# Attention and routed experts on one core: unscaled probabilities, the inverse sums spread by TensorE and applied to the output

## What is computed

```python
qkv = jnp.einsum('bsm,qhdm->bqhsd', x, W_qkv)
qk_rot = qk * cos + _rotate_half(qk) * sin
scores = jnp.einsum('bhqd,bhkd->bhqk', Q, K)
scores = jnp.where(causal, -jnp.inf, scores) / sqrt(DK)
attn = jax.nn.softmax(scores, axis=-1)
out = jnp.einsum('bhqk,bhkd->bhqd', attn, V)
out = out.transpose(0, 2, 1, 3).reshape(B, S, H * DK)
return jnp.einsum('bsh,dh->bsd', out, W_o)
...
x = x + _L0_attn_ref(xn, L0_attn_W_qkv, L0_attn_W_o) + _L0_ffn_ref(xn, ...)
```

## Time and profile before

| | |
|---|---|
| median of 3 runs | 1601.31 us (1599.42 to 1608.61) |
| profiled execution | 1614.56 us, span 1612.7 us |
| TensorE busy | 1267.3 us (79%) |
| VectorE busy | 1155.0 us (72%) |
| ScalarE busy | 1123.7 us (70%) |
| GpSimd busy | 971.7 us (60%) |
| granted TensorE clock, mean | 0.942 of full speed |

### The profile page before, as it was taken

How to read it: one execution, slowest core, us unless ns; L and a number is a source line. 1 busy time by engine, 2 the same in 40 slices (tenths; PEclk the granted TensorE clock), 3 DMA queues, 4 the chain that set the end, 5 groups by cost and what they waited for, 6 DMA issues and landing times.

```text
span 1612.7 us, 46469 instructions
## 1 busy us (share of the span) xinstructions
PE 1267.3 (79%) x13108; PEld 874.4 (54%) x13109; DVE 1155.0 (72%) x4320; ACT 1123.7 (70%) x3606; POOL 971.7 (60%) x1579
## 2 busy tenths in 40 slices
PE   2415877788778878878699999888888888888888
PEld 1303544455444545555498899655555555555555
DVE  6787766666666666667377777777778787877776
ACT  6415666666666767667588888777778777767777
POOL 3245676767677767677200000488778787878776
PEclk9657999999998999999799999999999999999999
DMA  9612222222231322222333323234333333433341
GB/s 288 182 42 63 66 67 65 66 59 72 61 69 44 67 64 65 66 65 67 102 84 85 88 85 85 65 85 96 72 72 74 72 74 74 95 76 75 78 95 33
DMA packets 115784, 129.10 MB, mean 80 GB/s; under 512 B 11568, under 2 KB 75312, under 8 KB 115376
## 3 DMA queue, kind: packets, MB, share of 16 engines
q1 hardware_dynamic: 107056, 110.26, 28.5%
q0 software_dynamic: 8576, 17.33, 3.7%
HBM read 28.85 MB, written 31.59 MB: 37 GB/s over the span
## 4 chain that ended last, share of the span: by engine, by line
POOL 30%; PE 20%; issue 18%; DMA 17%; DVE 11%; ACT 2%; DVEq 1%; POOLq 1%; ACTq 0%; SPq 0%
DMA sorted_x_dram<-stage,rows_at 11%; POOL probs L478 7%; POOL probs L479 7%; PE bank L1081 5%; PE bank L1082 5%; DMA stage<-sorted_y_dram,rows_at 5%; PE bank L1083 4%; POOL arena L462 4%; POOL stage L489 4%; POOL sorted_x_dram L483 3%; POOL arena L461 3%; PE bank L1162 1%; PE bank L1152 1%; PE bank L1216 1%; DVE arena L951 1%
## 5 line engine op out<-in xcount | busy, mean ns | idle before, releaser
L624 ACT ACTIVATE probs<-arena,neg_max 128x128 f32<-128x128 f32 (+1 forms) x1024 | 453.6, 446 | 186.9 <-DVE neg_max L951 178.5
L1162 PE MATMUL bank<-ident,probs 128*128 128x128 f32 x1536 | 276.1, 290 | 165.5 <-POOL probs L479 140.2
L478 POOL TENSOR_TENSOR probs<-probs,inv_total 128x128 f32<-128x128 f32 x512 | 217.1, 424 | 229.6 <-DVE inv_total L958 127.2
L1162 PEld LDWEIGHTS bank<-ident,probs 128*128 128x128 f32 x1536 | 174.9, 145 | 272.6 <-issue 136.1
L951 DVE CUSTOM_DVE_ANT_0 arena<-bank,causal 128x128 f32<-128x128 f32 (+1 forms) x1024 | 315.8, 345 | 2.7 <-PE bank L1152 2.7
L489 POOL DMA_INDIRECT stage<-sorted_y_dram,rows_at x128 | 134.5, 1050 | 263.1 <-DMA sorted_y_dram<-stage 241.4
L479 POOL TENSOR_SCALAR probs<-probs,inv_total 128x256 f32<-128x256 f32 x512 | 274.6, 536 | 0.0
L1152 PE MATMUL bank<-arena 64*128 64x128 f16 (+1 forms) x3072 | 177.1, 250 | 50.6 <-DVE neg_max L951 47.2
L969 DVE TENSOR_TENSOR arena<-bank,arena 128x256 f16<-128x256 f32 x256 | 106.5, 416 | 133.2 <-ACT arena L616 122.3
L624 ACT ACTIVATION_READ_ACCUMULATOR probs<-arena,neg_max 128x1 f32 x1024 | 194.5, 190 | 0.0
L611 ACT ACTIVATE probsT<-bank 128x384 f32<-128x384 f32 x384 | 184.3, 480 | 10.4 <-PE bank L1162 10.2
(11 more groups left out here) (149 smaller groups left out, 2971.4 us busy)
## 6 DMA issues: line engine op xcount, KB each, us to landing
arena<-arena SPq DMA_DIRECT2D x256, 256.0 KB, 5.1
arena<-sorted_x_dram SPq DMA_DIRECT2D x72, 128.0 KB, 2.2
sorted_y_dram<-stage SPq DMA_DIRECT2D x72, 128.0 KB, 1.8
sorted_x_dram<-arena SPq DMA_DIRECT2D x3, 2304.0 KB, 17.9
arena<-experts_dram SPq DMA_DIRECT2D x8, 512.0 KB, 5.1
out_dram<-acc SPq DMA_DIRECT2D x32, 128.0 KB
sorted_x_dram<-arena SPq DMA_DIRECT2D x1, 2368.0 KB, 19.1
sorted_x_dram<-stage,rows_at POOLq DMA_INDIRECT x128, 2.4
```

The costliest lines, as they stand in the source:

```text
L478: nc.gpsimd.tensor_tensor(p0, p0, inv_total[:, s % 4, 0:1].broadcast_to([P, P]), ALU.mult)
L624: last = nc.scalar.activation(probs[:, s % 4, at:at + w], masked[:, s % 2, at:at + w], ACT.Exp, bias=neg_max[:, s % 2, t:t + 1], scale=-1. ...
L1162: last = nc.tensor.transpose(TP[s % 2][:, k * P:(k + 1) * P], probs[:, s % 4, k * P:(k + 1) * P], ident[:])
```

## The change

Probabilities are no longer scaled. A transpose waits for the exponential alone. VectorE takes the reciprocal of the sums for a pair at once, four steps after its scores, and makes two f16 parts of it (high and low, times 64). TensorE multiplies each part, spread over 64 columns, by an f16 unit matrix, so that the inverse of a token's sum stands in PSUM in each of its head's 64 rows (`turn_sums`, eight products a pair). ScalarE copies the output to SBUF whole (`o_copy`), VectorE multiplies it by the inverse one step later (`o_scale`), and GpSimd splits it in two f16 parts after another step (`o_split`). The product with V moves from the end of the even step to directly behind the scores, with the spreading products behind it. The sends move to odd steps only, one gather moves from step 10 to 9, and the dispatch of rows is done in two halves, at steps 0 and 8. There are four buffers for masked scores instead of two.

```diff
-SEND_AT = [1, 3, 5, 7, 9, 11, 12, 14]
-GATHER_AT = [1, 3, 5, 7, 9, 10, 11, 13]
+SEND_AT = [1, 3, 5, 7, 9, 11, 13, 15]
+DISPATCH_AT = [0, 8]
+GATHER_AT = [1, 3, 5, 7, 9, 9, 11, 13]
-INV_LAG, T_LAG, OUT_LAG, PV_LAG, O_LAG = 2, 3, 4, 5, 6
+T_LAG, OUT_LAG, INV_LAG, PV_LAG, O_LAG, SCALE_LAG, SPLIT_LAG = 3, 4, 4, 5, 6, 7, 8
...
+        INV = [b[:, SEQ:2 * SEQ] for b in bank[6:8]]
...
-            def scale(G, s):
-                pool.wait_ge(inv_done, G + 1)
-                p0, p1 = probs[:, s % 4, 0:P], probs[:, s % 4, P:PW]
-                nc.gpsimd.tensor_tensor(p0, p0, inv_total[:, s % 4, 0:1].broadcast_to([P, P]), ALU.mult)
-                nc.gpsimd.tensor_scalar(p1, p1, inv_total[:, s % 4, 1:2], 1.0, ALU.mult, ALU.mult).then_inc(p_ready, 1)
+            def o_split(J, j, parity):
+
+                pool.wait_ge(o_scaled, J + 1)
+                nc.gpsimd.tensor_tensor(pause[:], half[:, 0:1], half[:, 0:1], ALU.add)
+                hi, lo = ot_hi[parity][:, j, :], ot_lo[parity][:, j, :]
+                nc.gpsimd.tensor_copy(hi, o_whole[:, j % 2, :]).then_inc(o_hi, 1)
+                pool.wait_ge(o_hi, J + 1)
+                nc.gpsimd.tensor_tensor(lo, o_whole[:, j % 2, :], hi, ALU.subtract).then_inc(o_done, 1)
...
+                    if sends:
+                        i = SEND_AT.index(s)
+                        if i % PER == 0:
+                            pool.wait_ge(send_ready, 2 * b + i // PER + 1)
+                        if not (at == OPENING and i == 0):
+                            pool.wait_ge(sent, 16 * (PER * TOP * b + i))
...
-            def o_high(G, s, parity):
-
-                act.wait_ge(pv_done, G + 1)
-                nc.scalar.activation(ot_hi[parity][:, s // 2, :], PV[s // 2 % 2], ACT.Copy).then_inc(o_hi, 1)
+            def o_copy(J, j):
+
+                act.wait_ge(inv_turned, J + 1)
+                if not (isinstance(J, int) and J < 2):
+                    act.wait_ge(o_done, J - 1)
+                nc.scalar.activation(o_whole[:, j % 2, :], PV[j % 2], ACT.Copy).then_inc(o_out, 1)
...
-                G = 16 * b + s
-                dve.wait_ge(s_ready, 8 * b + s // 2 + 1)
-                if not (at_fill and s < INV_LAG):
-
-                    invert(G - INV_LAG, s - INV_LAG)
+                if s % 2 == 0:
+                    dve.wait_ge(s_ready, 8 * b + s // 2 + 1)
+                    if not (at_fill and s < INV_LAG):
+
+                        invert(8 * b + (s - INV_LAG) // 2, (s - INV_LAG) % H // 2)
...
+                if s % 2 == 0 and not (at_fill and s < INV_LAG):
+                    split_inverse(8 * b + (s - INV_LAG) // 2, (s - INV_LAG) % H // 2)
...
+            def split_inverse(J, j):
...
+                nc.vector.tensor_scalar(hi, inv, W_SCALE, None, ALU.mult).then_inc(inv_hi, 1)
+                dve.wait_ge(inv_hi, J + 1)
+                nc.vector.scalar_tensor_tensor(lo, inv, W_SCALE, hi, ALU.mult, ALU.subtract).then_inc(inv_ready, 1)
...
-            def o_low(J, s, parity):
-                dve.wait_ge(o_hi, J + 1)
-                j = s // 2
-                nc.vector.tensor_tensor(ot_lo[parity][:, j, :], PV[j % 2], ot_hi[parity][:, j, :], ALU.subtract).then_inc(o_done, 1)
+            def o_scale(J, j):
+                dve.wait_ge(o_out, J + 1)
+                dve.wait_ge(inv_turned, J + 1)
+                nc.vector.scalar_tensor_tensor(o_whole[:, j % 2, :], INV[j % 2], UNSCALE, o_whole[:, j % 2, :],
+                                               ALU.mult, ALU.mult).then_inc(o_scaled, 1)
...
             def transposes(G, s, free):
-                pe.wait_ge(p_ready, G + 1)
+                pe.wait_ge(exp_done, G + 1)
...
+            def turn_sums(b, j):
+
+                pe.wait_ge(inv_ready, 8 * b + j + 1)
+                for t in range(TPS):
+                    for l in range(2):
+                        for i in range(2):
+                            of = inv_parts[:, l, 2 * j % SUMS + i, t:t + 1].broadcast_to([P, DK])
+                            last = mm(INV[j % 2][64 * i:64 * i + 64, t * P:(t + 1) * P], of, ident_h[:], start=(l == 0), stop=(l == 1))
+                last.then_inc(inv_turned, 1)
...
-                    pe.wait_ge(o_done, 8 * b + j - 1)
+                    pe.wait_ge(o_scaled, 8 * b + j - 1)
...
+                    if ends:
+                        attend(ended[0], ended[1] // 2, at)
+                        turn_sums(ended[0], ended[1] // 2)
```

More of the change, by code:

```diff
@@ L513, in sample @@
                         send(SEND_AT.index(s))
-                    if gathers:
-                        gather(GATHER_AT.index(s))
+                    for k in gathers:
+                        gather(k)
             def rest_of(b):
-                for lag in range(INV_LAG, 0, -1):
-                    scale(16 * b + 16 - lag, H - lag)
+                for s in range(H, H + SPLIT_LAG):
+                    if (s - SPLIT_LAG) % 2 == 1:
+                        o_split(8 * b + (s - SPLIT_LAG - 1) // 2, (s - SPLIT_LAG) // 2, b % 2)
             former_samples(pool, sample)
@@ L863, in tile_slots, with dispatch @@
                 return slots[:, first:first + n, :] if isinstance(first, int) else slots[:, bass.ds(first, n), :]
-            def dispatch(b):
+            def dispatch(b, part):
                 if not (isinstance(b, int) and b == 0):
-                    dve.wait_ge(sent, 16 * PER * TOP * b)
-                for t in range(PER):
+                    dve.wait_ge(sent, 16 * PER * (TOP * b + part - 1))
+                n = PER // 2
+                for t in range(n * part, n * part + n):
                     tile = b * PER + t
@@ L1185, in sample @@
                         scores(b, s, parity, at == OPENING)
+                    ended = (b, s - PV_LAG) if s > PV_LAG else (b - 1, s - PV_LAG + H)
+                    ends = ended[1] % 2 == 1 and not (at in FILLS and s <= PV_LAG)
+                    if ends:
+                        attend(ended[0], ended[1] // 2, at)
+                        turn_sums(ended[0], ended[1] // 2)
                     for kind, j, u, psum, n in beside(b, at, s):
```

110 lines of the change are left out of this document (60 added, 50 removed).

## The result

The changed kernel takes 1659.12 us (median of 4 runs, 1659.0 to 1665.9) against 1604.74 us for the kernel before in the same session: 1.035 times as long (95% interval 1.031 to 1.040). I had said 1584 us, within 1546 to 1626. The change made the kernel 3.5% slower and fell outside the range.

The account below looks back on a forecast made before the run. No engine was full; waits bound it: GpSimd's send-scaling-transpose chain in former samples, VectorE in the rope half. Latter +8, former -29, ends +4 gave -17 us, about 1584 us; overall range 1546 to 1626, forecast's own 1568 to 1598.

Parts of the forecast that it names:

- products that spread the inverse: TensorE, eight products per pair, 256 pairs: 0.31 us a group, 2.5 us a sample, on the path only where TensorE limits.
- every rival: Four other outcomes: waits go everywhere 0.16, sends bind 0.17, VectorE's even step decides 0.14, spreading products dear 0.11.
- Sum: Whole kernel: latter samples +8, former samples -29, ends +4, together -17 us on 1614.56 us, or -1.05%.
- Former sample: Each sample of the sending half: -1.8 us, from 41.0 to near 39.2 us.
- Latter sample: Each sample of the half without sends: +0.5 us, from 36.9 to near 37.4 us.
- Dear: Rival on TensorE's spreading products: 0.75 us a group instead of 0.31, kernel at 1612 us; chance 0.11.
- VectorE's even step: Rope half: forecast +0.2 us a pair, 5.0 us; as rival, up to 0.65 us a pair, 1640 us, chance 0.14.
- the gathers: One gather moves from step 10 to 9, odd-step gathers start later: set against each other at -0.3 us a sample.
- The part for the scale: VectorE's output multiplication, moved from an odd step into the even step inside the loop: some 0.35 us a pair.
- Ends: End of either half, where nothing hides the longer tail of copy, scale, split and output product: +2 us twice.
- the pairs at 10 and 12 of a former sample: Sign of a right forecast: these pairs take near 5 us, though send landings still last up to 6 us.
- two halves: Dispatch of rows in a former sample stays: four operations of 0.34 us, some 1.1 us in two halves.

Follow-up runs that it names:

- e9: Changed kernel with 24 tiny products put in once in the first sample, ahead of the former loop, loop bodies untouched: 0.992, 1597.7 us.
- e2: Changed kernel without the low part of the inverse in the spread, four spreading products a pair instead of eight: 0.992, 1595.5 us.
- e5: Kernel before with four unread products of nine columns by one ahead of each product with V: 1.004.
- e6: Kernel before with nine unread products of nine columns by one ahead of each product with V: 1.006, 1617.4 us.
- e11: Kernel e3 with VectorE's output scale moved to the next odd step and GpSimd's split one step later: 0.949, 1526.4 us.
- e3: Changed kernel with both loops over samples written out, with no jumps: 0.966, 1557.4 us.
- e13: Kernel e6 with 18 of its tiny products taken out of the first sample, ahead of the former loop: 1.046, 1678.5 us.
- e10: Kernel e2 with 19 tiny products put in once in the first sample, ahead of the former loop: 1.000.
- e4: Kernel before with both loops over samples written out, with no jumps: 0.971, 1566.1 us.

## Why the prediction was wrong

**The step that failed** is the bullet on the products that spread the inverse. It priced eight products a pair, 256 pairs, by their time on TensorE alone (0.31 us a group, and that part was right: 0.33 us), and so did every rival. The sum had no term for their number: 16 instructions a pair, with the waits 278 more in a body of two samples, in a program of which that body is run seven times in each half. Both bodies then touched 8 blocks of 256 instructions instead of 7 and were fetched anew at every jump: 61 us that the sum had at nothing.

What it costs, from the changed kernel against e9: a former sample 40.97 us against 38.84, a latter one 39.30 against 37.39, over 15 samples each 32 + 29 = 61 us, or 5.1 us at each of the twelve jumps. 4.9 us of that is seen directly as the two stands of TensorE; the clock at 0.50 behind them adds to it, and waits that the jump had anyway (VectorE's "issue" of 2.3 to 3.1 us at e9's latter jumps is gone in the changed kernel, where VectorE waits for the scores) take from it. What share each has wasn't taken apart.

The Trainium skill ("Runtime: NRT & Kernel Launch", section "Instruction fetch mechanics") could have warned me that a loop's size can cost. It says that instructions come in blocks of 16 KiB, 256 instructions, that TensorE's memory for them is 128 KiB (eight such blocks), and that a jump whose target isn't in the current window of two pages must wait for a DMA of it. The packets here are 2.38 MB / 145 = 16.4 KB, and the limit lies where eight blocks would put it, if one of the eight is taken by the block fetched ahead: seven stay, eight don't, and nine packets come per iteration. That last picture is my reading of the counts; no run tests it. As to the window of two, here bodies of seven blocks jumped back without a single packet (e2, e5, e6, e9), so for TensorE the measurement decides against it.

**What held.** e9 is the changed kernel without the penalty, and can be set against each term:

- *Sum.* -17 us forecast on the profiled execution's time; e9's is 1597.8 against 1614.56, -16.8 us. That they agree so closely is luck: these are single executions of two sessions. The medians of e9's session are 1597.72 and 1608.38, -10.7 us, and its ratio says -0.8%, forecast -1.05%.
- *Former sample* forecast 39.2 us, e9 38.8. *Latter sample* forecast 37.4, e9 37.4.
- *Spreading products* forecast 0.31 us a group; measured 1132.52 to 1132.85 and, in e9, 1251.91 to 1252.25: 0.33 and 0.34 us. Leaving half of them out, with both bodies loaded, changes nothing (e2 0.992, e9 0.992). "Dear" was wrong, and the spacing of 81 ns of the Trainium skill ("TensorE: Matmul & The Clock Gate", section "Back-to-back issue gap") isn't met here either (0.33 us for eight is 41 ns each).
- *VectorE's even step*, 5.0 us forecast for the pair at 4, +0.2 us for each of the pairs at 2 to 8. In e9 the scores of one latter sample, the pairs at 4, 6 and 8 and the start of 10:

```profile
1339.49 0.67 PE L1192 MATMUL bank<-arena 64*128 64x128 f16 x12
1344.75 0.67 PE L1192 MATMUL bank<-arena 64*128 64x128 f16 x12 [0.33 <-DVE neg_max L975]
1349.44 0.67 PE L1192 MATMUL bank<-arena 64*128 64x128 f16 x12 [0.33 <-DVE neg_max L975]
1354.59 0.67 PE L1192 MATMUL bank<-arena 64*128 64x128 f16 x12 [2.05 <-DVE neg_max L975]
```

  5.26, 4.69 and 5.15 us. Taken as means over the fourteen samples of the latter loop (distances between the starts of the scores), the pairs at 2 to 8 make 19.4 us against 18.1 before: +1.3 where I said +0.9. The pairs at 10 to 14 make 13.2 against 13.9, -0.7, which is what the sum had for them with the gathers (+0.9 - 1.3 - 0.3). The part for the scale, 0.35 x 4 = 1.4 us a sample, equals what e11 gives back in a latter sample (36.0 - 34.6), but not in the place where I put it: from e3 to e11 the pairs at 2 to 8 lose only 0.5 us, and those at 10 to 14 lose 0.8, beside the shorter waits for gathered rows. In a former sample 0.5 comes back, and nothing of it in the pairs at 2 to 8. So 0.35 us a pair for the scale is not confirmed.
- *Ends* were under-priced: +4 us forecast. From the last former to the first latter sample 284.3 us against 280.6, and from the last sample's mark to the end 39.6 against 35.1: +8 us, paid for by the former samples.

**What was right in sum and wrong in place.** I expected the pairs at 10 and 12 of a former sample near 5 us. GpSimd no longer holds TensorE, but the second half of the dispatch now stands in the even step 8. VectorE there, in e9:

```profile
537.12 0.41 DVE L1008 SCALAR_TENSOR_TENSOR o_whole<-bank,o_whole 128x256 f32<-128x256 f32 x1
537.46 1.10 DVE L894 TENSOR_SCALAR stage<-acc,neg_mean,rstd 128x128 f32 x2
538.48 0.15 DVE L897 COPY rows_at<-slots 128x4 int32 x1
538.55 0.28 DVE L975 CUSTOM_DVE_ANT_0 arena<-bank,causal 128x128 f32<-128x128 f32 x1
```

```profile
539.24 1.14 PE L1192 MATMUL bank<-arena 64*128 64x128 f16 x12 [3.08 <-DVE neg_max L975]
```

The mask comes 1.1 us later, TensorE stands 3.08 us, and the twelve products then take 1.14 us instead of 0.67:

```profile
539.20:544.80 5.60, 5.56 (x41) 3.73 (x42) 2.45 (x13) 3.43 (x12) 3.07 (x6) 0.50 0.26 47
```

The granted clock is at 0.50 again. The pair at 8 takes 6.2 us and that at 10 7.1, the one at 12 then 4.4; before, those at 10 and 12 took 5.7 and 8.4. As means over the fourteen samples of the former loop, the pair at 8 takes 6.2 us (4.7 before), that at 10 5.9 (5.6), that at 12 4.4 (7.6). I had counted the dispatch by its sum, "two halves", and not asked in which step its second half would land.

**Still open:** whether a loop of other lengths has the same edge; what size VectorE's loop would need to lose its stand at the jumps; and which instruction exactly is at the cut. Loops kept and the scale in the odd step together gave no result, so whether e11's gain adds to e9's isn't known.

## What to carry to other kernels

Before an edit adds instructions to a loop, count the loop's instructions on that engine in the trace and look at the packets of the instruction queue: if none fall inside the loop now, the edit may have a second price, which is not its duration. An "issue" wait at a loop's head, within a group of products that waits for nobody, together with instruction packets once per iteration, is its signature; here moving the loop by some 50 instructions (e9), or writing it out (e3), removed it. Look at every engine: in the kernel before it was VectorE that stood behind each jump. When a result misses a sum whose terms all look right, move or straighten the loop first and measure the terms after that.

## What the runs showed of the hardware

- Here TensorE's loop body stayed loaded when it touched seven blocks of 256 instructions and was fetched anew, with nine packets of 16 KB an iteration, when it touched eight with 38 or more in the last (by cuts at 178 + 256 n, fitted to these loops): 5 us a jump in the changed kernel. The same 1684 instructions are in one case or the other by where they begin (e9), and so are 1680 (e6, e13).
- A body with 6 or 7 instructions in the eighth block by the same cuts was fetched anew at one jump of six in the profiled execution (e10).
- Behind a pause of 5.1 us with 0.29 us of work, and behind one of 3.08 us, the granted clock was at 0.50, for 4.6 and 5.6 us in the windows shown.
- Writing out both loops gave the kernel before 3% and the changed kernel 2.5% on top of e9 (1597.7 to 1557.4 us), although neither e9 nor the kernel before fetched TensorE's body anew. Of the 42 us in the kernel before, 34 us are seen as VectorE's stands behind the twelve jumps, which e4 doesn't have.
